# Attention head products shared between GpSimd and VectorE in a two-layer gated transformer kernel: the last tile of each chunk moves to VectorE, with keys and values in PSUM

## The reference

```python
def _L0_xattn_ref(Q, K, V, Wq, bq, Wk, bk, Wv, bv, Wo, bo):
    N, L, HID, EMB, NH = (4, 512, 128, 128, 16)
    HD = EMB // NH
    q = (Q @ Wq.T + bq).reshape(n, ql, NH, HD)
    k = (K @ Wk.T + bk).reshape(n, K.shape[1], NH, HD)
    v = (V @ Wv.T + bv).reshape(n, V.shape[1], NH, HD)
    attn = jnp.einsum('nlhd,nled->nlhe', q, k) / jnp.sqrt(jnp.asarray(HD, q.dtype))
    attn = jax.nn.softmax(attn, axis=-1)
    ctx = jnp.einsum('nlhe,nled->nlhd', attn, v)
    return ctx.reshape(n, ql, NH * HD) @ Wo.T + bo
```

## Time and profile before

| | before |
|---|---|
| median of 3 runs | 1520.16 us (1517.12 to 1520.34) |
| the profiled execution | 1511.0 us, span 1509.2 us |
| PE busy | 1171.4 us, 78% |
| DVE busy | 1021.7 us, 68% |
| POOL busy | 775.4 us, 51% |
| ACT busy | 552.1 us, 37% |
| DMA | 178.79 MB, mean 118 GB/s |

### The profile page before, as it was taken

The page is one execution under the profiler, slowest core; times in us unless marked ns, Lnnn a source line. Parts: engine busy times, 40 slices in busy tenths (PEclk is TensorE's granted clock), DMA queues, the critical chain, the costliest instruction groups (busy, mean ns, idle before and its releaser), DMA issues.

```text
span 1509.2 us, 23312 instructions
## 1 busy us (share of the span) xinstructions
PE 1171.4 (78%) x7704; PEld 1011.4 (67%) x7704; DVE 1021.7 (68%) x2488; ACT 552.1 (37%) x1196; POOL 775.4 (51%) x383
## 2 busy tenths in 40 slices
PE   2332234898878888788787899999988888888887
PEld 1222223787768777587676889889877777777776
DVE  2888777777767877677733544546677777777776
ACT  1321111443424444244334254453344444434442
POOL 5999998898878999789932001011011111111100
PEclk9955556998879999899998999999999999999999
DMA  8510115665656665565555244442000000000000
GB/s 285 202 50 24 31 35 198 219 198 170 193 188 203 197 201 194 191 204 180 198 180 186 98 146 150 137 154 88 18 22 22 22 22 22 22 22 22 22 8 15
DMA packets 120679, 178.79 MB, mean 118 GB/s; under 512 B 8696, under 2 KB 79472, under 8 KB 120560
## 3 DMA queue, kind: packets, MB, share of 16 engines
q1 hardware_dynamic: 115440, 164.71, 33.8%
q0 software_dynamic: 5120, 12.59, 2.6%
HBM read 136.37 MB, written 40.89 MB: 117 GB/s over the span
## 4 chain that ended last, share of the span: by engine, by line
PE 49%; DVE 17%; POOL 15%; issue 8%; ACT 5%; DMA 2%; SPq 2%; DVEq 0%; POOLq 0%; ACTq 0%
PE YB L1239 10%; POOL prod L560 10%; PE YD L1271 4%; PE ZD L1196 3%; PE ZD L1198 3%; PE ZD L1197 3%; DVE s L817 3%; PE ZB L1196 3%; POOL prod L572 3%; PE ZB L1198 3%; PE ZB L1197 3%; PE MC L1192 3%; ACT xn L639 2%; PE YB L1271 2%; POOL xs L582 2%
## 5 line engine op out<-in xcount | busy, mean ns | idle before, releaser
L547 POOL TENSOR_TENSOR rstd<-ve,neghalf 128x4 f32<-128x4 f32 x32 | 32.9, 1028 | 560.7 <-DVE ve L801 560.7
L657 ACT ACTIVATE hid<-ZB,w2b 128x256 f32<-128x256 f32 x480 | 189.2, 474 | 348.1 <-PE ZB L1198 346.5
L560 POOL TENSOR_TENSOR prod<-q_sb,kv_sb 128x2048 f32<-128x2048 f32 x64 | 286.9, 4507 | 23.0 <-DVE q_sb L839 11.8
L572 POOL TENSOR_TENSOR prod<-s,kv_sb 128x2048 f32<-128x2048 f32 x64 | 287.9, 4521 | 20.4 <-ACT s L673 19.7
L1239 PE MATMUL YB<-w2b,hid 128*128 128x128 f32 x1920 | 271.4, 300 | 7.5 <-ACT hid L657 7.5
L1239 PEld LDWEIGHTS YB<-w2b,hid 128*128 128x128 f32 x1920 | 251.4, 211 | 36.7 <-issue 17.9
L817 DVE TENSOR_REDUCE s<-prod 128x256 f32<-128x2048 f32 x64 | 146.0, 2281 | 61.2 <-POOL prod L560 60.2
L839 DVE TENSOR_REDUCE q_sb<-prod 128x128 f32<-128x2048 f32 x64 | 145.9, 2280 | 18.6 <-POOL prod L572 18.5
L1196 PE MATMUL ZB<-bt_hi,w1b 128*128 128x256 f32 x480 | 147.9, 308 | 1.6 <-ACT hid L657 1.6
L679 ACT ACTIVATE su<-ZD 128x512 f32<-128x512 f32 x101 | 60.7, 601 | 231.6 <-PE ZD L1198 230.2
L1197 PE MATMUL ZB<-bt_hi,w1b 128*128 128x256 f32 x480 | 136.9, 285 | 0.0
...
## 6 DMA issues: line engine op xcount, KB each, us to landing
...
```

Of the source, the lines that this page charges most:

```text
L560: pool.tensor_tensor(out=prod[:, t % 2, :].rearrange("p (h e d) -> p h e d", h=HEADS, e=HEADS), in0=q.unsqueeze(2).broadcast_to([P, HEADS, ...
L572: pool.tensor_tensor(out=prod[:, t % 2, :].rearrange("p (h d e) -> p h d e", h=HEADS, e=HEADS), in0=s0[:, t, :, :].unsqueeze(2).broadcast_ ...
L657: act.activation(hid[n % 2][:, j, :], ZB[j // 2][:, (j % 2) * RT:(j % 2 + 1) * RT], ACT.Relu, bias=w2b[t % 2][:, e, FJ * D + j:FJ * D + j ...
```

## The change

POOL multiplies only tiles 0 to 2 of a chunk (`PT` = 3). DVE multiplies tile 3, into a buffer of its own, `own_prod`, with keys and values in PSUM: half a bank of ZD1 per chunk, `kv_own`, chunks in turn. DVE makes the q-k product in tick 3 behind the norm statistics and the product with values in tick 6. DVE and ACT are kept apart in that bank: ACT's copy into it waits for DVE's q-k product of the chunk before, and DVE's product with values waits until ACT's copy of the next chunk is done. POOL's scatters move from tick 0 to tick 3, behind its third product. The halves of `prod` change sides between keys and values.

All biases of the first attention are added by PE, as two matmuls of a row of ones with the high and the low part of the bias in the rounded fp32r type, so that ACT takes keys, values and queries out of PSUM by plain copies. The old bias matmul of "wo" (L1288) goes. In layer 1 "lv" goes: its matmuls accumulate into "val", and DVE adds the bias there once instead of two additions. The conversion of weights uses ZB in place of ZD.

```diff
@@ bank uses
-C_LATER = {0: "xt2", 1: "sc", 2: "lv", 4: "val", 5: "att", 7: "xt3"}
+C_LATER = {0: "xt2", 1: "sc", 4: "val", 5: "att", 7: "xt3"}
...
+        kv_own = [ZD[1][:, i * 2 * D:(i + 1) * 2 * D] for i in range(2)]
...
@@ sync
                         if has(c - 1):
-                            filled(sp, "lv", c - 1)
+                            filled(sp, "val", c - 1)
@@ gpsimd: times_k, times_v, the ticks
-                if t < 2:
-                    if has(a - 1):
-                        pool.wait_ge(av_sum.sem, av_sum.at(a - 1, 3 + t))
-                else:
-                    pool.wait_ge(score0.sem, score0.at(a, t - 1))
+                if t == 2:
+                    pool.wait_ge(score0.sem, score0.at(a, 1))
+                elif has(a - 1):
+                    pool.wait_ge(av_sum.sem, av_sum.at(a - 1, 2 + t))
...
                 if t < 2:
-                    pool.wait_ge(score0.sem, score0.at(a, 3 + t))
+                    pool.wait_ge(score0.sem, score0.at(a, 2 + t))
                 else:
-                    pool.wait_ge(av_sum.sem, av_sum.at(a, t - 1))
+                    pool.wait_ge(av_sum.sem, av_sum.at(a, 1))
...
-                    if k < 4:
+                    if k < PT:
                         times_k(a, k)
-                    else:
+                    if 4 <= k < 4 + PT:
                         times_v(a, k - 4)
-                if k == 0 and has(r - 1):
+                if k == 3 and has(r - 1):
                     scatter(r - 1)
@@ scalar
+            def keys_values(p, half):
+
+                b = filled(act, f"kv{half}", p)
+                n = PT - 2 if half else 2
+                last = act.activation(kv_sb[p % 2][:, 2 * half:2 * half + n, :].rearrange("p j d -> p (j d)"), b[:, 0:n * 2 * D], ACT.Copy)
+                if half:
+                    if has(p - 1):
+                        act.wait_ge(own_qk.sem, own_qk.at(p - 1))
+                    last = act.activation(kv_own[p % 2], b[:, n * 2 * D:2 * 2 * D], ACT.Copy)
+                last.then_inc(free_of(f"kv{half}", p), 1)
...
+                if k == 3 and has(p):
+                    keys_values(p, 0)
                 if k == 4:
                     if has(p):
+                        keys_values(p, 1)
...
+                if k == 6 and has(p):
+                    plain(q_sb[p % 2][:, :, :].rearrange("p j d -> p (j d)"), "q", p)
...
@@ vector
+            def own_times_k(a):
+
+                emptied(dve, "q", a)
+                q = q_sb[a % 2][:, PT, :].rearrange("p (h d) -> p h d", h=HEADS)
+                kk = kv_own[a % 2][:, 0:D].rearrange("p (e d) -> p e d", e=HEADS)
+                dve.tensor_tensor(out=own_prod[:].rearrange("p (h e d) -> p h e d", h=HEADS, e=HEADS),
+                                  in0=q.unsqueeze(2).broadcast_to([P, HEADS, HEADS, HD]),
+                                  in1=kk.unsqueeze(1).broadcast_to([P, HEADS, HEADS, HD]),
+                                  op=ALU.mult).then_inc(own_qk.sem, 1)
+
+            def own_times_v(a):
+                dve.wait_ge(exp0.sem, exp0.at(a, 2))
+                if has(a + 1):
+                    emptied(dve, "kv1", a + 1)
...
@@ vector, the ticks
-                    if has(p):
-                        keys_values(p, 0)
+                    if has(a):
+                        own_times_k(a)
...
-                    if has(p):
-                        keys_values(p, 1)
...
-                    if has(p):
-                        queries(p)
+                        own_times_v(a)
...
-                    if kc == 2:
-                        biased(BLV, lv_sb, "lv", c)
                     if kc == 4:
-                        b = filled(dve, "val", c)
-                        dve.tensor_tensor(out=u_sb[:], in0=tiles(b), in1=lv_sb[:], op=ALU.add).then_inc(free_of("val", c), 1)
+                        biased(BLV, u_sb, "val", c)
@@ tensor
+            def bias_rows_of(dst, at, n, times):
+
+                out_ = dst.rearrange("p (j d) -> p j d", j=times)
+                for n_, part in enumerate((bias_hi, bias_lo)):
+                    pe.matmul(out_, ones_r[:], part[:, at:at + n].unsqueeze(1).broadcast_to([1, times, n]), start=(n_ == 0), stop=False)
...
-                        pe.matmul(b[:], ones[0:1, :], brow[0:1, BO:BO + D].unsqueeze(1).broadcast_to([1, TILES, D]), start=True, stop=False)
+                        bias_rows_of(b[:, :], BO, D, TILES)
...
-                        by_token(b, ctx_t, WKV, 2 * D, (2 * half, 2 * half + 1)).then_inc(full(name, c), 1)
+                        bias_rows_of(b[:, :], BKV, 2 * D, 2)
+                        by_token(b, ctx_t, WKV, 2 * D, (2 * half, 2 * half + 1), start=False).then_inc(full(name, c), 1)
...
-                        by_token(b, xt0, WQ, D).then_inc(full(name, c), 1)
+                        bias_rows_of(b[:, :], BQ, D, TILES)
+                        by_token(b, xt0, WQ, D, start=False).then_inc(full(name, c), 1)
...
-                if name == "lv":
-                    by_token(b, ctx2_t, WLV, D).then_inc(done, 1)
...
-                        last = pe.matmul(b[:, j * P:(j + 1) * P], blockdiag[:, j, :], vv_sb[:, j, :], start=True, stop=True)
+                        js = slice(j * P, (j + 1) * P)
+                        pe.matmul(b[:, js], ctx2_t[:, js], ws[:, WLV:WLV + D], start=True, stop=False)
+                        last = pe.matmul(b[:, js], blockdiag[:, j, :], vv_sb[:, j, :], start=False, stop=True)
```

52 lines of the change are left out of this document (37 added, 15 removed).

## The result

The changed kernel takes **1539.0 us** (median of 4 runs, 1537.92 to 1539.89) against 1519.4 us for the kernel before in the same session. The ratio is 1.0131, with a 95% interval of 1.0113 to 1.0148. The forecast was 1474 us, with a range of 1446 to 1508. The profiled execution took 1539.9 us (span 1538.1) where the sum of the prediction gives 1465.

What follows compares the result with a forecast made beforehand. GpSimd was taken as the bound without experts, and as fullest with TensorE close behind among expert steps. Gains of 23.2 + 23.0 + 0 = 46 us took 1520.2 to 1474 us, range 1446 to 1508.

Steps and rivals of the forecast that it cites:

- Products: Attention: two of eight products per chunk move to VectorE at 2.3 us each; GpSimd loses 9.0 us per chunk.
- Rival D: VectorE's product is dear, up to 4.5 us each, making the kernel slower at 1544 us; chance 0.08.
- Chunks without experts: Chunks 0 to 3: VectorE becomes the bound, chunks 2 and 3 fall from 85.2 to 70.6 us; gain 23.2 us.
- Chunks with experts: Usual chunks among expert steps fall from 45.15 to 42 us, TensorE at 40.5 leaving no room below; gain 23.0 us.
- Biases: TensorE's added bias matmuls in the attention: +0.8 us per chunk, between 0 and +1.5.
- rival B: Expert ticks are paced by TensorE and VectorE handing each other tiles, GpSimd's wait only an echo: 1501 us; chance 0.18.
- Evictions: Bank copies move from VectorE (2.03 us less per chunk) to ScalarE's free time; queue place adds 0.5 us at most.
- The block ends: First three block ends: moved scatters delay the sorted tile's transpose by 5.7 us; net gain over these chunk pairs 0.
- After the attention: Part after the attention: lv's lost bias addition against its moved matmuls, between -10 and +3 us, taken as 0.
- Rival E: The moved scatter holds SP's (SyncE's) queue in every chunk, with expert weights behind it: 1516 us; chance 0.07.

Runs made afterwards that it cites:

- e3: Changed kernel with VectorE again taking out the banks and adding the biases of queries, keys and values, without their bias matmuls: 1538.8 us, ratio 1.0128.
- e6: Changed kernel with six more bias matmuls per chunk on TensorE, adding zero, from chunk 5 on: 1566.0 us.
- e13: Changed kernel's scheme before chunk 5, earlier scheme with third product buffer and lv apart after; TensorE bias matmuls from chunk 6, VectorE adding zeros: 1488.6 us, ratio 0.9842.
- e4: Changed kernel with scatters behind the first product, lv apart, and VectorE adding biases and taking banks out; VectorE's products stay: 1528.1 us, ratio 1.0060.
- e15: e11 with ScalarE normalising the attended row ahead of its copies from chunk 6 on: 1493.0 us, ratio 0.9872.
- e14: e11 without the bias matmuls of queries, keys and values from chunk 6 on, those biases missing from its result: 1476.3 us, ratio 0.9752.
- e11: Changed kernel with lv apart and, from chunk 5, eight products on GpSimd (third buffer) and scatters behind the first: 1515.6 us, ratio 0.9987.
- e5: Changed kernel with only the scatters of a block's last chunk issued behind the first product again: 1519.3 us, ratio 1.0006.
- e2: Changed kernel with lv again having its own matmuls, bank and bias addition: 1535.0 us, ratio 1.0094.
- e10: Kernel before, with GpSimd's last-tile product in a third buffer and the output projection's bias in the rounded type: 1489.4 us, ratio 0.9813.

## Why the prediction was wrong

By medians it is off by 65 us (1539.0 against 1474), by profiled executions by 74.9 (1539.9 against 1465), mostly since the one before was so far below its median. The stretches say where: block-end pairs 30.9, pairs of usual expert chunks 32.4 (the last one counted up to the first vv_sb), the start 4.8, after the attention 6.9.

- ***Products* was right**: 2.276 us for 2.3, and nothing extra for PSUM. The 62 fixed cycles by which a reader of PSUM exceeds one of SBUF in the Trainium skill ("VectorE: DVE Perf Modes", "The TRN2 errata", 120 against 58) don't show: the reduction that reads own_prod from SBUF takes 2.278, though it is another instruction. Rival D is out.
- ***Chunks without experts* was right** for chunks 2 and 3, with VectorE busy 68.9 of 70.6 us; that the sum came out to the decimal is luck, they take 36.6 and 34.0. The "about 30" for chunk 0 had no working behind it: it took 32.2, and chunk 1 gained 1.1. The first product came at 26.45 us instead of about 22.3: three pairs of bias matmuls stand in that path, 1.1 us each before the chunk's own matmul can start, and ScalarE's split copies, and I had charged 0.9 for all. Without both it comes at 21.66 (e3).
- ***Chunks with experts* failed**, and with it the most. I added VectorE's busy time and its leftover waits and called TensorE's 40.5 us a floor. But TensorE has its own sum, and its waits did not go: at 0.96 of the clock busy 39.0 to 39.7 plus 5.5 of waits was the chunk before, and 41.0 plus 4.9 is the chunk now. That a chunk is busy time plus waits is so for every engine; that this sum is the one that counts is seen from e6 and e13, where more of TensorE lengthens the chunks, and from e3 and e4, where less of GpSimd does not shorten them. That VectorE's leftover waits were only the echo of TensorE's is argued and not shown. *Biases* was mis-sized too: at 0.96 of the clock TensorE went from 39.0 to 41.0 us, +1.9 for my +0.8 and my upper end of +1.5, and in e6 and e13 such matmuls cost at least about their length. This is rival B's mechanism, and dearer than B was priced: B kept 45 us, the chunks took 45.8 to 50.3.
- ***Evictions* failed** at ScalarE's "0.5 us at most". I looked at one wait, the copy's for VectorE's product, and not at the normalisations and relus that now stand behind four more instructions in each chunk. e15 shows that this place matters (17 us) where TensorE adds the biases too; without the bias matmuls (e14) the copies cost 10 us, not clear of noise.
- ***The block ends* was right up to the transpose and failed behind it.** From the end of the tables to the transpose I forecast 20.3 us, and it took 19.8 (210.4 to 230.2); then 8.3 to the end of the statistics, and it took 8.6. The last term, 16 us to the second output sum, took 23 (238.9 to 261.7): the relus come late at ScalarE, the copies stand ahead of the normalisations, and the pick behind those. How the 7 us are shared among these no run shows; they seem to come with the copies and bias matmuls, and not with VectorE's products: e11's block ends, with the former alone, are as long as e5's (60.1, 58.3, 58.5), and e4's, with the latter alone, are 52.6, 54.9 and 54.8. The moved scatter itself, forecast at 5.7 us, costs 6.6 (e5: 20 us for three).
- ***After the attention*** came out at +6.9, past its bounds of -10 and +3. I had weighed VectorE's addition against lv's matmuls and not seen that TensorE, with less ahead of its wait for hu, loses its clock more often (e2); that accounts for the late chunks, not for all of the 6.9 us.
- Rival E's mechanism (SyncE's queue) didn't decide: apart from the 11.1 us ahead of its first instruction, TensorE's waits in the changed kernel name no load of expert weights.

What stays open is why two chunks alike in work differ in whether the clock falls, late ones and those among expert steps (chunk 10 of the changed kernel takes 45.9 us at 0.96, chunk 11 takes 50.3 at 0.86, with 292 matmuls each); the runs show how often it does, not what decides it. Open too is the third buffer's share in e10, as it was never run without the rounded bias.
